# Attention scores as f32 products of four padded heads, and a generator built in four parts

## The chip, the cores and the metric

The kernel runs on one core of one Trainium2 chip. Its time is the device time of one execution in microseconds (us); the median of a few runs counts. The engines are TensorE (PE), VectorE (DVE), ScalarE (ACT) and GpSimd (POOL); SyncE (SP) issues most transfers. Each works through its own list in order, and semaphores tie the lists together.

## The reference

Two blocks follow each other on x of 16 sequences x 128 positions x 144 channels (C), with a condition vector of 144 for each sequence.

```python
# block 1: adaptive layer norm, attention with H = 16 heads of D = 9, MLP with FF = 576
ada = silu(c) @ W_ada + b_ada        # six vectors of 144 a sequence
h = layernorm(x) * (1 + scale_msa) + shift_msa
q, k, v = split(h @ W_qkv + b_qkv)
o = softmax(q * D**-0.5 @ k.T) @ v   # for each of the 16 heads
x = x + gate_msa * (o @ W_proj + b_proj)
h = layernorm(x) * (1 + scale_mlp) + shift_mlp
x = x + gate_mlp * (gelu(h @ W_fc1 + b_fc1) @ W_fc2 + b_fc2)
# block 2: rotation in the column space of P (144 x 64)
U, _ = qr(P)
A = skew(silu(cond) @ W.T + b)       # 64 x 64 from 2016 entries, for each sequence
z = x @ U
x = x + (z @ expm(A) - z) @ U.T
```

## The kernel before, in words

All weights and x stay in on-chip memory (SBUF). After a setup of about 33 us (loads, transposed W, the six vectors) one list of iterations b = -2 to 17 runs on every engine, each in four quarters q = 0 to 3. It is a software pipeline: iteration b transposes the input of sequence b + 2, makes q, k and v of b + 1 (`qkv`), the scores of b (`scores`), the exponentials and values of b - 1 (`scores_T`, `values`), and closes b - 2 (`sums`, `division`, `projection`, `gated`). Two other computations are threaded through the same iterations:

- **The QR of P**, as 64 steps of elimination on a matrix Z, four an iteration in 0 to 15. A step is a pair of products on TensorE that copy a row of Z to all partitions (`G_row` L1308, `B_row` L1313, with a selector that POOL makes), and nine small VectorE instructions (`eliminations`, L908 to L928), which use a root made by POOL. The next step's rows can only be made when Z is updated.
- **The matrix exponential of A**: entries (`windows` L1179, 252 tiny passes in iterations -1 and 0), `triangles`, `generator`, `scaled`, powers in iterations 2 to 4, halves in 5, odd part in 6, four squarings in 7 to 10 (`product`, L1171).

Scores: q and k are split into three bf16 parts and laid out in 64 columns a head (`qs`, `ks`), two heads a stack, transposed by TensorE (`stacks_T`, L1255) and copied by ScalarE (L622, L626). `scores` (L1263) forms four heads a quarter into one PSUM bank; VectorE takes their maximum (L984); the 16 maxima are again split in three and transposed (`NM`). `scores_T` forms the same scores transposed (L1273) and adds the negative maximum by a second product (L1274); ScalarE takes the exponential (L616). `values` (L1284) multiplies by v in 32-column groups. `sums` (L1292) adds the exponentials, VectorE takes 128 reciprocals (L944), `division` (L1300) spreads them, VectorE multiplies (L949), `projection` (L1318) ends it. Scores and transposed scores have a bank each (3 and 4).

```python
                for i in range(4):
                    dst = bank[4][:, 128 * i:128 * i + 128]
                    mm(dst, KT[parity][q // 2][:, q % 2, i, :], QT[parity][q // 2][:, i, :], start=True, stop=False)
                    ins = mm(dst, headsel[:, q % 2, 4 * (q // 2) + i, :], NMT[:, :], start=False, stop=True)
                ins.then_inc(s_ST, 1)
```

An f32 product appears as two TensorE instructions (passes) in the trace, a bf16 product or a transpose as one. After iteration 17 comes a last stage: M = expm(A) U^T, the MLP and the rotation.

## Time and profile before

| | us |
|---|---|
| median of 3 runs | 362.62 (361.86 to 363.21) |
| the profiled execution, its own time | 363.15 |
| its span, first to last instruction | 361.4 |
| TensorE busy | 318.2 (88%) |
| VectorE busy | 256.6 (71%) |
| ScalarE busy | 187.2 (52%) |
| POOL busy | 146.2 (40%) |
| mean granted TensorE clock | 0.948 of 2.4 GHz |

Busy time counts a matmul until its last result is in PSUM; matmuls overlap, so the distance between two starts tells what one costs in a stream, and the duration what a single reader waits for. What a stage costs is read by stretches of the span. The granted clock has two levels, 1.2 and 2.4 GHz, shown as 0.5 and 1.0 of full speed.

### The profile page before, as it was taken

The numbers are of one execution on the slowest core, as the hardware profiler recorded it, in microseconds if no ns is written. First come the engines' busy times: TensorE is split into PE (matmuls) and PEld (weight loads), VectorE is DVE, ScalarE is ACT, GpSimd is POOL, SyncE is SP. The second block draws the span as 40 slices with busy tenths as digits, with TensorE's granted clock in tenths as the row PEclk, the third lists the DMA queues.
The fourth block names the chain that finished last, engine by engine and source line by source line (L and its number), as shares of the span: only waits on it lengthen the run. The fifth ranks groups of instructions, "written<-read, shape, count | busy, mean of one in ns | idle before, by whom it ended". The sixth has DMA issues, their size and how long they took to land.

```text
span 361.4 us, 10608 instructions
## 1 busy us (share of the span) xinstructions
PE 318.2 (88%) x3935; PEld 245.4 (68%) x3935; DVE 256.6 (71%) x1063; ACT 187.2 (52%) x403; POOL 146.2 (40%) x421
## 2 busy tenths in 40 slices
PE   0598989889989899999999999999987957999995
PEld 0472668567877788787778777777776643467784
DVE  7381036688899989887786878988988576664243
ACT  1222464347766557567685676776762233623221
POOL 3512124235355454553543535545543508720000
PEclk9998765769999999999999999999999899999999
DMA  8817000000000000000000000000000000000013
GB/s 198 233 19 261 4 1 2 3 1 2 2 3 2 2 5 3 2 2 3 2 3 2 5 2 2 0 5 0 2 3 3 2 3 0 2 0 2 0 34 100
DMA packets 8765, 8.28 MB, mean 23 GB/s; under 512 B 1042, under 2 KB 8312, under 8 KB 8586
## 3 DMA queue, kind: packets, MB, share of 16 engines
q1 hardware_dynamic: 8006, 6.78, 6.5%
q10 hardware_dynamic: 708, 0.83, 0.8%
q8 instruction: 32, 0.52, 0.6%
q14 instruction: 19, 0.16, 0.2%
HBM read 6.40 MB, written 1.20 MB: 21 GB/s over the span
## 4 chain that ended last, share of the span: by engine, by line
PE 61%; DVE 18%; ACT 8%; issue 5%; POOL 4%; DMA 2%; ACTq 1%; DVEq 0%; POOLq 0%
PE bank L1255 5%; PE bank L1492 5%; PE bank L1284 4%; PE bank L1476 3%; PE bank L1318 3%; PE bank L1171 3%; PE bank L1273 3%; PE bank L1308 3%; PE bank L1300 3%; PE bank L1244 3%; PE bank L1245 2%; PE bank L1179 2%; PE bank L1274 2%; ACT KT L626 2%; PE bank L1263 2%
## 5 line engine op out<-in xcount | busy, mean ns | idle before, releaser
L440 POOL TENSOR_TENSOR root<-rec,mhalf 128x1 f32<-128x1 f32 x64 | 34.6, 540 | 107.5 <-DVE Z L922 107.5
L984 DVE TENSOR_REDUCE nmax<-bank 128x4 f32<-128x512 f32 x64 | 43.0, 672 | 34.5 <-PE bank L1263 34.2
L616 ACT ACTIVATE E<-bank 128x512 f32<-128x512 f32 x64 | 38.0, 594 | 40.6 <-PE bank L1274 40.2
L626 ACT ACTIVATE KT<-bank 64x512 bf16<-64x512 bf16 x64 | 37.5, 587 | 0.8
L1273 PE MATMUL bank<-QT,KT 128*128 128x128 bf16 x256 | 36.7, 224 | 0.0
L1274 PE MATMUL bank<-NMT,headsel 128*128 128x128 bf16 x256 | 36.3, 222 | 0.0
L1308 PE MATMUL bank<-Z,sel 128*128 128x128 f32 x128 | 29.5, 314 | 6.9 <-DVE Z L928 6.8
L1284 PE MATMUL bank<-E,V 128*32 128x128 f32 x512 | 27.9, 291 | 5.4 <-ACT E L616 5.4
L622 ACT ACTIVATE QT<-bank 128x512 bf16<-128x512 bf16 x32 | 19.0, 595 | 26.1 <-PE bank L1255 26.0
L1273 PEld LDWEIGHTS bank<-QT,KT 128*128 128x128 bf16 x256 | 24.3, 99 | 10.0 <-issue 10.0
L1308 PEld LDWEIGHTS bank<-Z,sel 128*128 128x128 f32 x128 | 20.9, 200 | 14.7 <-issue 13.6
L1263 PE MATMUL bank<-KT,QT 128*128 128x128 bf16 x256 | 25.8, 225 | 0.3 <-DVE nmax L984 0.3
L1274 PEld LDWEIGHTS bank<-NMT,headsel 128*128 128x128 bf16 x256 | 25.4, 99 | 0.2
L1313 PE MATMUL bank<-Z,sel 128*128 128x64 f32 x128 | 22.3, 257 | 1.3 <-DVE Z L928 1.3
L922 DVE SCALAR_TENSOR_TENSOR Z<-bank,cG,Z 128x128 f32<-128x128 f32 x64 | 22.2, 346 | 0.0
L1313 PEld LDWEIGHTS bank<-Z,sel 128*128 128x128 f32 x128 | 20.4, 201 | 1.4 <-DVE Z L928 1.4
L1300 PE MATMUL bank<-rsum,sumrow 128*128 128x128 f32 x128 | 18.5, 288 | 1.5 <-DVE rsum L944 1.5
L928 DVE SCALAR_TENSOR_TENSOR Z<-bank,cB,Z 128x64 f32<-128x64 f32 x64 | 18.2, 284 | 2.3
L434 POOL COPY sel<-ident 128x128 f32<-128x128 f32 x64 | 19.4, 305 | 0.0
L1318 PE MATMUL bank<-wproj,ON 128*128 128x144 f32 x128 | 19.1, 293 | 0.0
L1300 PEld LDWEIGHTS bank<-rsum,sumrow 128*128 128x128 f32 x128 | 15.5, 191 | 4.7 <-issue 3.0
L1492 PE MATMUL bank<-wfc2a,gT 128*128 128x144 f32 x128 | 18.6, 288 | 0.0
(270 smaller groups left out, 827.5 us busy)
## 6 DMA issues: line engine op xcount, KB each, us to landing
gates<-gates_dram SPq DMA_DIRECT2D x1, 2304.0 KB, 8.4
x_all<-in_x_dram SPq DMA_DIRECT2D x4, 288.0 KB, 7.6
out_dram<-x_all SPq DMA_DIRECT2D x8, 144.0 KB, 2.0
wskew<-in_L_cond_W_dram SPq DMA_DIRECT2D x4, 283.5 KB
wada<-in_L_cond_W_ada_dram ACTq DMA_DIRECT2D x1, 432.0 KB
wfc1a<-in_L_cond_W_fc_dram SPq DMA_DIRECT2D x1, 288.0 KB
wfc2a<-in_L_cond_W_fc_dram SPq DMA_DIRECT2D x1, 288.0 KB
wproj<-in_L_cond_W_proj_dram SPq DMA_DIRECT2D x16, 5.1 KB
```

What stands on the lines that cost most here:

```text
L440: link(nc.gpsimd.tensor_tensor(root[:, at], rec[:, at], mhalf[:, 0:1], ALU.pow))
L616: nc.scalar.activation(E[:, q, :, :].rearrange("p i t -> p (i t)"), bank[4][:, :], ACT.Exp).then_inc(s_E, 1)
L626: nc.scalar.activation(KT[parity][n][own, p, :, :].rearrange("p g t -> p (g t)"), bank[2][own, 256:512].bitcast(BF16), ACT.Copy).then_inc( ...
L984: nc.vector.tensor_reduce(nmax[:, q % 2, 4 * (q // 2):4 * (q // 2) + 4], bank[3][:, :].rearrange("p (i m) -> p i m", i=4), AX.X, ALU.max, ...
L1263: ins = mm(bank[3][:, 128 * i:128 * i + 128], QT[parity][q // 2][:, i, :], KT[parity][q // 2][:, q % 2, i, :], start=True, stop=True)
L1273: mm(dst, KT[parity][q // 2][:, q % 2, i, :], QT[parity][q // 2][:, i, :], start=True, stop=False)
L1274: ins = mm(dst, headsel[:, q % 2, 4 * (q // 2) + i, :], NMT[:, :], start=False, stop=True)
L1284: ins = mm(bank[5][own, cols], V[parity][:, head(q, i), :], E[:, q, i, :], start=True, stop=True)
L1300: ins = mm(bank[6][:, 128 * q:128 * q + 128], sumrow[:, q, :], rsum[:, :], start=True, stop=True)
L1308: mm(bank[7][:, 0:2 * RD], sel[:, n, :], Z[:, 0:2 * RD], start=True, stop=True).then_inc(s_Grow, 1)
L1313: mm(bank[7][:, 2 * RD:3 * RD], sel[:, n, :], Z[:, 2 * RD:3 * RD], start=True, stop=True).then_inc(s_Brow, 1)
L1492: mm(dst, gT[Q % 2][:, k, cols], wfc2a[:, k, :], start=(k == 0), stop=False)
```

## The change

- q and k are no longer split. Each head gets 32 columns (`SL`) in f32, four heads a stack. Column D of a head's k is 1; column D of q takes the negative maximum, so one product gives score minus maximum. `keys_T`, `queries_T` and, once the maxima are there, `queries_again_T` transpose four stacks each in f32. `scores` and `scores_T` make eight heads at a time, each head a product of 32 rows in its own row group and its own bank out of 0 to 3; both use the same four banks. VectorE takes two maxima of 1024 elements, ScalarE two exponentials of 1024, an iteration.
- v gets a column of ones, so that `values` yields the sums too. `sums` and `division` go; the result is transposed back (`heads_back`), divided in 16 reciprocals and one product (`divided`), transposed (`normalized_T`) and projected with two products instead of four.
- The elimination starts in iteration -2: four steps in -2, -1 and in even iterations, three in odd ones, one B step left in 16 (`STEPS`). Its products read the identity matrix instead of selectors. They share bank 7 with `heads_back` and `projection`, which therefore wait for the last step (`row_bank`).
- The entries of A are formed in four parts in iterations 0 to 3 (`windows(n)`, `triangles(n)`), the generator in 4, its scaling in 5, `any_over` and the powers from 6, halves in 9, odd part in 10, squarings in 11 to 14. All of it uses banks 4 and 5, which are also those of the stacks, so TensorE waits in `bank5_read` and `bank4_read` until they are read.
- POOL's selectors, its subtractions and its spreading of v go; `column_cleared` comes. POOL's addition of sequence b - 3 and its statistics move to quarter 0 of iteration b. W_proj is loaded by 3 transfers instead of 17, and 8 small setup operations go.
- ScalarE's order in an iteration is now: `queries_again`, `modulated`, the copy of the values, `stacked` (q, k, v), the first exponential, `keys_copied`, `queries_copied`, the generator's copies, the copies of the transposed output, the second exponential.

VectorE's order is now: maximum 0, step 0, statistics (quarter 0); step 1, `divided`, powers' sums (1); maximum 1, step 2, `normalized`, the generator's work (2); step 3, `gated` (3).

```diff
-    SL = 64
-    NP6 = 6 * D
+    SL = 32
...
+        qstk = [sb(f"qstk{p}", [128, H, SL]) for p in range(2)]
+        kstk = sb("kstk", [128, H, SL])
+        QT, QM = sb("QT", [128, 4, 128]), sb("QM", [128, 4, 128])
+        KT = [sb(f"KT{p}", [128, 4, 128]) for p in range(3)]
+        V = [sb(f"V{p}", [128, H, VS]) for p in range(3)]
+        E = sb("E", [128, 2, 4, 2, 128])
...
+        STEPS = {}
+        for b in range(-2, B + 1):
+            for q in range(4):
+                if len(STEPS) <= RD and (b < 0 or q < 3 or b % 2 == 0):
+                    STEPS[b, q] = len(STEPS)
+        assert len(STEPS) == RD + 1
...
+        PARTS, POWER, HALVES, ODD, SQUARE = 4, 6, 9, 10, 11
...
+            def column_cleared(b):
+                pool.wait_ge(s_qmT, b + 1)
+                nc.gpsimd.memset(qstk[b % 2][:, :, D:D + 1], 0.0).then_inc(s_qz, 1)
             def added(b):
-                wait(pool, s_pr, b + 2, s_apart[0])
-                xb = x_all[:, bass.ds(b, 1), :].rearrange("p a c -> p (a c)")
-                nc.gpsimd.tensor_tensor(xb, xb, tmp[:, :], ALU.add).then_inc(s_x1, 1)
+                pool.wait_ge(s_pr, b + 1)
+                nc.gpsimd.tensor_tensor(x_all[:, b, :], x_all[:, b, :], tmp[:, :], ALU.add).then_inc(s_x1, 1)
...
+            def queries_again(b):
+                act.wait_ge(s_qmT, b + 1)
+                wait(act, s_ST, 2 * b)
+                nc.scalar.activation(QM[:, :, :].rearrange("p j t -> p (j t)"), bank[5], ACT.Copy).then_inc(s_QM, 1)
...
+            def exponentials(b, g):
+                act.wait_ge(s_ST, 2 * b + g + 1)
+                wait(act, s_pv, 2 * b - 1 + g)
+                nc.scalar.activation(E[:, g, :, :, :].rearrange("p r j t -> p r (j t)"), scored(g), ACT.Exp).then_inc(s_E, 1)
...
+            def triangles(n):
+                first, last = 16 * n, min(16 * n + 16, RD - 1)
+                dve.wait_ge(s_LP, n + 1)
+                TT(A0[:, :, first:last].rearrange("p c i -> p i c"),
+                   bank[5][:, 0:(last - first) * NC].rearrange("p (i c) -> p i c", c=NC),
+                   lower[:, first:last].rearrange("p (i a) -> p i a", a=1).to_broadcast([128, last - first, NC]),
...
+            def maximum(b, g):
+                dve.wait_ge(s_S, 2 * b + g + 1)
+                wait(dve, s_qmT, b - 1)
+                nc.vector.tensor_reduce(qstk[b % 2][:, 8 * g:8 * g + 8, D:D + 1].rearrange("p (j r) a -> p r (j a)", r=4),
+                                        scored(g).rearrange("p r (j m) -> p r j m", j=2),
+                                        AX.X, ALU.max, negate=True).then_inc(s_max, 1)
...
+            def windows(n):
+                first, last = 16 * n, min(16 * n + 16, RD - 1)
+                pe.wait_ge(s_v, 4)
+                pe.wait_ge(s_KT, n + 2)
...
+            def generator_stage(b):
+                if 0 <= b < PARTS:
+                    windows(b)
+                if b == PARTS:
+                    pe.wait_ge(s_L, PARTS)
+                    pe.wait_ge(s_KT, b + 2)
+                    matrices_T(A0, 5, s_LTp)
+                if b == PARTS + 1:
+                    norms(b)
+                if b == PARTS + 2:
+                    any_and_replicas(b)
+                if power(b):
+                    powers(b)
+                if b == HALVES:
+                    high_halves(b)
+                if b == ODD:
+                    odd_part(b)
+                if squaring(b):
+                    squared(b)
...
+            def bank5_read(b):
+                wait(pe, s_KT, min(b + 2, B))
+                if 0 <= b < PARTS:
+                    pe.wait_ge(s_L, b + 1)
+                if b == PARTS:
+                    pe.wait_ge(s_rsq, 1)
+                if b == PARTS + 1:
+                    pe.wait_ge(s_Bs, 1)
+                if power(b):
+                    pe.wait_ge(s_N, b - POWER + 1)
+                if b == HALVES:
+                    pe.wait_ge(s_ev, 6)
+                if b == ODD:
+                    pe.wait_ge(s_X, 1)
+                    pe.wait_ge(s_Y, 1)
+                if squaring(b):
+                    pe.wait_ge(s_X, b - SQUARE + 2)
...
+            def stack_T(dst, stack, done):
+                for j in range(4):
+                    ins = pe.transpose(dst[:, 128 * j:128 * j + 128], stack[:, 4 * j:4 * j + 4, :].rearrange("p h s -> p (h s)"),
+                                       ident[:, :])
+                ins.then_inc(done, 1)
+            def keys_T(b):
+                pe.wait_ge(s_stk, 2 * b + 2)
+                wait(pe, s_QM, b - 1)
+                if b == 0:
+                    pe.wait_ge(s_v, 3)
+                stack_T(bank[5], kstk, s_kT)
+            def queries_T(b):
+                pe.wait_ge(s_stk, 2 * b + 2)
+                pe.wait_ge(s_V, b + 1)
+                wait(pe, s_qz, b - 1)
+                stack_T(bank[4], qstk[b % 2], s_qT)
+            def queries_again_T(b):
+                pe.wait_ge(s_max, 2 * b + 2)
+                stack_T(bank[5], qstk[b % 2], s_qmT)
...
+            def scores(b, g):
+                pe.wait_ge(s_QT, b + 1)
+                pe.wait_ge(s_KT, b + 1)
+                wait(pe, s_max, 2 * b + g)
+                wait(pe, s_E, 2 * b - 2 + g)
+                if b == 0:
+                    pe.wait_ge(s_v, 4)
+                for j in range(2):
+                    for r in range(4):
+                        rows = slice(32 * r, 32 * r + 32)
+                        ins = mm(bank[r][:, 128 * j:128 * j + 128], QT[rows, 2 * g + j, :], KT[b % 3][rows, 2 * g + j, :],
+                                 start=True, stop=True)
                 ins.then_inc(s_S, 1)
...
+            def scores_T(b, g):
+                pe.wait_ge(s_QM, b + 1)
+                pe.wait_ge(s_max, min(2 * b + 3 + g, 2 * B))
+                wait(pe, s_E, 2 * b + g)
+                for j in range(2):
+                    for r in range(4):
+                        rows = slice(32 * r, 32 * r + 32)
+                        ins = mm(bank[r][:, 128 * j:128 * j + 128], KT[b % 3][rows, 2 * g + j, :], QM[rows, 2 * g + j, :],
+                                 start=True, stop=True)
                 ins.then_inc(s_ST, 1)
...
+            def row_bank(k, b):
+                wait(pe, s_Gstep, min(k, RD))
                 wait(pe, s_Bstep, k - 1)
-                mm(bank[7][:, 0:2 * RD], sel[:, n, :], Z[:, 0:2 * RD], start=True, stop=True).then_inc(s_Grow, 1)
-            def B_row(k, n):
-                wait(pe, s_Bstep, k)
-                mm(bank[7][:, 2 * RD:3 * RD], sel[:, n, :], Z[:, 2 * RD:3 * RD], start=True, stop=True).then_inc(s_Brow, 1)
+            def heads_back(b):
+                pe.wait_ge(s_O, b + 1)
+                wait(pe, s_pr, b)
+                for n in range(2):
+                    cols = slice(128 * n, 128 * n + 128)
+                    ins = pe.transpose(bank[7][:, 256 + 128 * n:384 + 128 * n], Osb[:, cols], ident[:, :])
+                ins.then_inc(s_Ot, 1)
+            def normalized_T(b):
+                pe.wait_ge(s_on, b + 1)
+                pe.transpose(bank[5][:, 0:128], ON[:, 0:C1], ident[:, :])
+                pe.transpose(bank[5][0:C2, 128:256], ON[:, C1:C], ident[:, :]).then_inc(s_OnT, 1)
             def projection(b):
-                pe.wait_ge(s_on, b + 1)
-                for q in range(4):
-                    ins = mm(bank[6][:, 0:C], ON[:, q, :], wproj[:, q, :], start=(q == 0), stop=(q == 3))
-                ins.then_inc(s_proj, 1)
+                pe.wait_ge(s_oT, 2 * b + 2)
+                mm(bank[7][:, 256:256 + C], oT1[:, :], wproj1[:, :], start=True, stop=False)
+                mm(bank[7][:, 256:256 + C], oT2[:, :], wproj2[:, :], start=False, stop=True).then_inc(s_proj, 1)
...
+            def step(b, q, before=None):
+                k = STEPS.get((b, q))
+                if k is not None or before:
+                    last = k if k is not None else max([n for at, n in STEPS.items() if at < (b, q)]) + 1
+                    row_bank(last, b)
+                if before:
+                    before(b - 2)
+                if k is None:
+                    return
+                if k < RD:
+                    mm(bank[7][:, 0:2 * RD], ident[:, k:k + 1].to_broadcast([128, 128]), Z[:, 0:2 * RD],
+                       start=True, stop=True).then_inc(s_Grow, 1)
+                if k > 0:
+                    mm(bank[7][:, 2 * RD:3 * RD], ident[:, k - 1:k].to_broadcast([128, 128]), Z[:, 2 * RD:3 * RD],
+                       start=True, stop=True).then_inc(s_Brow, 1)
...
+            def attention(b):
+                if scoring(b):
+                    scores(b, 0)
+                if b >= 3:
+                    pe.wait_ge(s_pr, b - 2)
+                step(b, 0)
+                if closing(b):
+                    values(b - 2, 1)
+                if b == B + 1:
+                    transposed_again(0)
+                if prepares(b):
+                    qkv(b + 1)
+                if b == -1:
+                    generator_entries(3, 4)
+                if weighing(b):
+                    scores_T(b - 1, 0)
+                step(b, 1, heads_back if closing(b) else None)
+                if b == B + 1:
+                    transposed_again(1)
+                if prepares(b):
+                    keys_T(b + 1)
+                    queries_T(b + 1)
+                if b == B:
+                    U_parts(b, 0)
+                if scoring(b):
+                    scores(b, 1)
+                if weighing(b):
+                    values(b - 1, 0)
+                generator_stage(b)
+                if b == B:
+                    U_parts(b, 1)
+                if closing(b):
+                    pe.wait_ge(s_on, b - 1)
+                step(b, 2)
+                if closing(b):
+                    bank5_read(b)
+                    normalized_T(b - 2)
+                if b == B + 1:
+                    more_squarings()
+                    transposed_again(2)
+                if weighing(b):
+                    scores_T(b - 1, 1)
+                step(b, 3, projection if closing(b) else None)
+                if b == B + 1:
+                    transposed_again(3)
+                if scoring(b):
+                    if closing(b):
+                        pe.wait_ge(s_oT, 2 * b - 2)
+                    else:
+                        bank5_read(b)
+                    queries_again_T(b)
+                if normalizing(b):
+                    if b > -2:
+                        bank4_read(b)
+                    inputs_T(b + 2)
```

## Rows read from the trace of the kernel before

**Rows 1.** The page: busy time of TensorE; its granted clock in 40 slices

```profile
PE 318.2 (88%) x3935; PEld 245.4 (68%) x3935; DVE 256.6 (71%) x1063; ACT 187.2 (52%) x403; POOL 146.2 (40%) x421
...
PEclk9998765769999999999999999999999899999999
```

**Rows 2.** Stretches: start:end, us; busy us (instructions) of each engine; granted clock, DMA

```profile
47.10:63.30 16.20, 15.41 (x180) 12.66 (x178) 9.19 (x40) 8.40 (x18) 6.35 (x21) 0.61 0.01 2
63.30:82.80 19.50, 16.45 (x152) 12.01 (x151) 14.95 (x64) 7.65 (x18) 6.36 (x18) 0.71 0.01 2
...
95.90:110.70 14.80, 13.34 (x202) 10.87 (x200) 14.41 (x56) 9.80 (x22) 7.78 (x22) 1.00 0.01 3
...
154.20:214.10 59.90, 56.97 (x928) 47.47 (x925) 45.84 (x196) 41.62 (x93) 27.45 (x88) 1.00 0.01 2
214.10:265.80 51.70, 48.56 (x670) 39.46 (x667) 45.41 (x196) 36.70 (x83) 27.36 (x88) 1.00 0.01 2
265.80:299.00 33.20, 24.33 (x325) 19.18 (x326) 25.32 (x111) 10.88 (x21) 11.32 (x30) 0.95 0.01 2
```

**Rows 3.** The page's groups: line, operation, shapes, count; busy us, mean ns; idle before

```profile
L984 DVE TENSOR_REDUCE nmax<-bank 128x4 f32<-128x512 f32 x64 | 43.0, 672 | 34.5 <-PE bank L1263 34.2
L616 ACT ACTIVATE E<-bank 128x512 f32<-128x512 f32 x64 | 38.0, 594 | 40.6 <-PE bank L1274 40.2
...
L1318 PE MATMUL bank<-wproj,ON 128*128 128x144 f32 x128 | 19.1, 293 | 0.0
```

**Rows 4.** Timeline of TensorE in iteration 12: start us, us, operation, count

```profile
227.08 0.96 PE L1244 MATMUL bank<-wqkv,hT 128*128 128x432 f32 x2
...
228.60 0.45 PE L1308 MATMUL bank<-Z,sel 128*128 128x128 f32 x2
...
229.15 0.43 PE L1284 MATMUL bank<-E,V 128*32 128x128 f32 x8
229.39 1.06 PE L1292 MATMUL bank<-E,sumsel 128*32 128x128 f32 x32
230.38 0.23 PE L1273 MATMUL bank<-QT,KT 128*128 128x128 bf16 x1
...
230.84 0.39 PE L1263 MATMUL bank<-KT,QT 128*128 128x128 bf16 x4
231.06 0.44 PE L1308 MATMUL bank<-Z,sel 128*128 128x128 f32 x2
```

**Rows 5.** Timeline of TensorE in the last stage

```profile
306.40 1.02 PE L1476 MATMUL bank<-hT1q,wfc1a 128*128 128x512 f32 x2
...
307.57 1.14 PE L1482 MATMUL bank<-hT2q,wfc1r 17*128 17x512 f32 x8
...
350.60 0.66 PE L1504 MATMUL bank<-ident,x_all 128*128 128x128 f32 x4
351.09 0.27 PE L1505 MATMUL bank<-ident,x2r 128*128 128x128 f32 x1
```

**Rows 6.** Timeline of VectorE: an elimination's first instruction and what follows the elimination

```profile
229.26 0.17 DVE L908 RECIPROCAL rec<-bank 128x1 f32<-128x1 f32 x1
...
230.79 0.95 DVE L944 RECIPROCAL rsum<-bank 128x128 f32<-128x128 f32 x1
```

**Rows 7.** Timeline of TensorE in iterations -1 and 0

```profile
34.63 0.99 PE L1244 MATMUL bank<-wqkv,hT 128*128 128x432 f32 x2 [0.98 <-ACT hT L547]
...
46.80 0.63 PE L1263 MATMUL bank<-KT,QT 128*128 128x128 bf16 x4
47.22 1.75 PE L1244 MATMUL bank<-wqkv,hT 128*128 128x432 f32 x2
...
50.21 0.61 PE L1308 MATMUL bank<-Z,sel 128*128 128x128 f32 x2
50.74 1.10 PE L1179 MATMUL bank<-ident,v 16*64 16x8 f32 x32
```

**Rows 8.** VectorE's instructions grouped by line

```profile
L934 DVE TENSOR_TENSOR tmp<-bank,gates 128x144 f32<-128x144 f32 x16 | 4.8, 298 | 1.8 <-PE bank L1318 1.8
```

683 lines of the change are left out of this document (240 added, 443 removed).

## The prediction

> **What bounds the kernel now.** I read the page's busy times first: TensorE 318.2 us of 361.4, and its clock row, which shows where the granted clock was low [rows 1]. Then the busy times in stretches cut at the iterations [rows 2]. Iterations 0 to 14 take 218.7 us (47.1 to 265.8), iterations 15 to 17 take 33.2 us, the last stage 62.4 us, which the change leaves alone. In iterations 11 to 14 one takes 51.7 / 4 = 12.9 us, TensorE 94% busy, VectorE 88%; with squarings (7 to 10) 59.9 / 4 = 15.0 us. So TensorE sets the pace there and VectorE is close behind. Iterations 0 and 1 are dearer, 16.2 and 19.5 us: waits behind the generator, at a mean granted clock of 0.61 and 0.71.
>
> The timeline gives the price of each kind of product by starts, not by durations, which overlap [rows 4]: qkv 1.52 us; G and B rows 0.55 with the change of array shape behind them; four values products 0.24; 16 sums products 0.99, of which 0.85 is streaming and 0.14 the change back to full shape; eight bf16 products of scores_T 0.46; four of scores 0.22.
>
> **TensorE, per iteration.** *Removed:* sums, 0.99; division, four f32 products of 128 columns at 0.21 (below) and a change of shape, 1.0; half of the projection, 19.1 / 16 = 1.19 for eight passes [rows 3], so 0.5 saved; 32 bf16 products of scores_T (4 x 0.46 = 1.84), 16 of scores (0.88), 17 bf16 transposes at 0.055 (0.94). *Added:* 12 f32 transposes of stacks, four of heads and outputs. Four f32 transposes take 0.49 by starts, 0.66 with a tail of 0.17 [rows 5], so 0.12 each: 16 cost 1.8. The scores are now 16 f32 products with 32 rows, and scores_T 16 more. No such row exists, and two bounds stand around it. Bound above: each f32 product of 128 columns costs what one of full shape costs; a 512-column one takes 1.02 for its two passes, 0.85 without the tail [rows 5], so 128 columns 0.21, and 32 cost 6.8 us. Bound below: four in different row groups run at once. The nearest row speaks for that: L1482 does four products of 17 rows by 128, 512 columns, each into its own bank, in 1.14 us where one alone takes 1.02 [rows 5]. That is the new pattern itself, with other columns. I take 0.43 for eight, 1.7 for all 32. Values stay at 0.85. Changes of array shape go from 8 to about 11, at 0.1 to 0.14 each: +0.4. Sum: 12.1 busy before (94% of 12.9), less 6.2 removed, plus 1.8 + 1.7 + 0.4: **9.9 us**.
>
> The Trainium skill (TensorE: Matmul & The Clock Gate, "Measured speedup vs the span model") gives 3.07x, not 4x, for four row tiles. By that the 32 products would cost 2.2 us instead of 1.7, an estimate that would add under 0.5 us per iteration if all of it lay on the path. The trace agrees that there is an overhead, but shows 12% (1.14 against 1.02).
>
> **VectorE becomes the pace.** One elimination takes 1.53 us from its first instruction to the next work (229.26 to 230.79) [rows 6], and needs rows that TensorE makes only when the one before has finished. A maximum over 512 elements takes 0.67 [rows 3]; one over 1024 is bounded by 0.67 and 1.34; I take 1.15. The maxima's three-way split (four small operations) and the 128-wide reciprocal (0.95 [rows 6]) go; a reciprocal of 16 and a product of 144 remain, 0.55 together. The chain of an iteration with four steps: maximum 1.15, elimination 1.53, wait until TensorE has passed values, qkv, scores_T and heads_back and made the next rows 1.25, elimination 1.53, division 0.55, maximum 1.15, elimination 1.53, xn 0.3, wait for projection and rows 0.85, elimination 1.53, gated 0.3 (298 ns [rows 8]), less overlaps: **11.6**. With three steps it ends over TensorE: projection 0.5, queries_again_T 0.45, inputs_T 0.2, scores 0.45 and changes of shape behind the third elimination: **10.9**. Mean 11.25 against 12.9. ScalarE loses the copies of the bf16 split and keeps three stack copies of 512 columns out of six; its exponentials are two of 1024 elements, about 1.05 each (594 ns for 512 [rows 3]). That fits the gaps. POOL loses selectors and subtractions; VectorE's work hid them, so they give nothing. New waits: `statistics` now waits for POOL's addition, queued there behind a root and a masked column; that ends inside the 1.25 us in which VectorE waits for rows anyway, and would cost 0.3 outside it. `wait(s_pr)` ahead of step 0 holds values and qkv behind it, but gated ends before the maximum that covers it. SP's queue is shorter by 14 small weight loads, so the gates behind them land sooner; nothing on the path waits for them.
>
> **The generator's work now meets closed waits.** `bank5_read` stands ahead of `normalized_T`, so TensorE waits at once for what VectorE does at the end of quarter 2, and scores_T, projection and the fourth step are queued behind it. On top of 11.6 / 10.9: windows of 64 passes cost 2.1 (32 passes 1.1 [rows 7]) and triangles 0.3, before the third elimination: iterations 2 and 3 come to 14.6 and 13.7; 0 and 1, which close nothing, to 12.3 each. The generator's three operations (about 2 us) wait in full: 15.3 in iteration 4; scaling, 13.9 in 5. Powers add 1 us of TensorE, and first and second power 3 us of VectorE (14.41 busy in 95.9 to 110.7 against 45.41 / 4 = 11.35 [rows 2]): 12.7, 13.7, 14.8 in 6 to 8. Halves and odd part, 14.7 and 14.5. Squaring, 2 us of TensorE, delays the third elimination by 1.5: 12.6 mean in 11 to 14. Sum 24.6 + 28.3 + 29.2 + 41.2 + 29.2 + 50.4 = **202.9 against 218.7: -15.8**.
>
> **Start.** Eight eliminations move ahead of iteration 0, none of them covered. Each costs 1.53 plus 0.6 for its rows: four delay xn and the first hT, so qkv(0) comes at about 41.6, not 34.6 [rows 7]. The other four overlap qkv and the last entries. With four steps of 2.1 to 2.2 us, qkv and the last entries at the lower clock (3.0 and 3.4), and transposes, I get the first scores at 54, not 46.8: **+7**; with overlap of the entries at best +3. ScalarE's and POOL's setup (the headsel copy, KT memsets) was off this path.
>
> **End.** Iteration 15 has three steps and no preparation: 10.5. In 16 one B step is left; behind it U's parts and the 14-wide root as now; 17 is shorter by the 128-wide reciprocal and division. About 26.5 for all three against 33.2 [rows 2]: **-6.7**.
>
> Sum: 361.4 - 15.8 + 7 - 6.7 = 345.9. TensorE now has gaps of 2 to 4 us in iterations 2 to 10. The trace shows what the lower clock does: iterations 0 and 1, where TensorE waits or issues the tiny window products, have a granted clock of 0.61 and 0.71 of 2.4 GHz, and qkv takes 2.99 us (47.22 to 50.21) instead of 1.52 [rows 2, 4, 7]. At 1.2 GHz the pieces on the path (projection, queries, scores, rows) cost up to 2.2 more per iteration. I allow two or three such iterations beyond those of now, +5: span 350.9. The profiled run lies 1.75 above its span, the median 0.5 below that run: **352**.
>
> **Rivals.**
> *The clock* (ends slower). TensorE stays at 1.2 GHz through most of iterations -2 to 10. For: its idle share rises from 6% to 15 to 20%, and iterations 0 and 1 had 0.61 and 0.71. Against: iteration 3's stretch has 10% idle and 1.00. At 2.2 us each it decides from seven iterations on (347.1 + 7 x 2.2 = 362.5); twelve give 373. The Trainium skill (TensorE: Matmul & The Clock Gate, Part 1) says that idleness lets the clock fall to 1.2 GHz. Chance 0.17.
> *No overlap of row groups.* 6.8 instead of 1.7 us, 16 times 5.1 = 82, perhaps 15 hidden in gaps: 415. Against it stands L1482. 0.06.
> *The four shared banks.* Scores and scores_T use the same four banks four times an iteration, each after a maximum or an exponential; where these don't fit the gaps another 1 us per iteration is lost: 362 to 368. Before, scores and scores_T had a bank each. 0.10, half of it within 0.5%.
> *More.* The waits between eliminations overlap better and the clock holds: 1 us less per iteration, 330 to 340. 0.12.
> *Forecast:* 0.55, its own range 341 to 361.
>
> A difference under 0.5% (1.8 us) can't be told from none. Faster: 0.53 + 0.12 + 0.01; same: 0.08; slower: 0.26. The range leaves out the no-overlap case and half of the clock's: 338 to 370.
>
> **What would show it.** Right: eight scores products in about 0.6 us with their tail; TensorE busy under 90% in 11 to 14, with iterations of 12.6 us and its waits on VectorE; first scores near 54; waits of TensorE for VectorE ahead of projection and normalized_T. Wrong: scores passes that start 0.1 us apart; a clock under 0.85 over the span; iterations 0 and 1 over 14 us.

## The result and the profile after

379.25 us, median of 4 runs (378.27 to 379.55), against 362.38 of the kernel before beside it: ratio 1.046, 95% interval 1.043 to 1.049. 352 was forecast, within 338 to 370. The profiled execution took 379.3 us, span 377.5. In all ratios below, executions over 1.5% above a kernel's fastest are left out as slow: three of e3's four and two of e12's seven.

The page of the changed kernel: busy time of the engines and the granted clock in 40 slices.

```profile
PE 304.5 (81%) x3471; PEld 221.1 (59%) x3471; DVE 227.7 (60%) x966; ACT 130.4 (35%) x274; POOL 92.6 (25%) x279
...
PEclk9978587887696988899999696999999986999999
```

Every engine is busy for less time than before [rows 1] and the kernel takes longer. The clock row says where to look: dips up to slice 25 and at 33 and 34, where before they ended with slice 9 but for one. The mean granted clock is 0.890, before 0.948; as the engine has two levels (1.2 and 2.4 GHz), that is 2 x 0.110 x 377.5 = 83 us at the lower one against 2 x 0.052 x 361.4 = 38.

The same execution cut at the first scores of iterations 0, 2, 6, 9, 11 and 15 and at the first product of the last stage: start:end, us; busy us (instructions) of each engine; granted clock, DMA.

```profile
56.70:84.80 28.10, 23.66 (x305) 18.35 (x304) 18.97 (x86) 8.16 (x18) 7.19 (x25) 0.80 0.01 2
84.80:153.80 69.00, 55.67 (x703) 42.67 (x702) 39.72 (x164) 23.96 (x53) 14.05 (x49) 0.80 0.01 2
153.80:195.50 41.70, 35.05 (x511) 26.57 (x510) 31.47 (x127) 19.59 (x43) 10.45 (x36) 0.99 0.01 2
195.50:231.60 36.10, 28.77 (x373) 22.12 (x372) 21.39 (x87) 12.23 (x27) 7.41 (x26) 0.83 0.01 1
231.60:285.70 54.10, 49.54 (x799) 38.35 (x798) 34.76 (x149) 27.97 (x60) 14.33 (x50) 0.99 0.01 2
285.70:314.20 28.50, 17.35 (x233) 12.33 (x232) 20.34 (x96) 9.55 (x19) 10.23 (x25) 0.89 0.01 1
314.20:377.50 63.30, 58.63 (x412) 39.95 (x412) 31.55 (x100) 20.25 (x41) 16.78 (x33) 0.96 0.07 20
```

Against the terms of the prediction (its sum 345.9, before the 5 us allowed for the clock):

| stretch | forecast | measured | off |
|---|---|---|---|
| to the first scores | 54 | 56.7 | +2.7 |
| iterations 0, 1 | 24.6 | 28.1 | +3.5 |
| 2 to 5 | 57.5 | 69.0 | +11.5 |
| 6 to 8 | 41.2 | 41.7 | +0.5 |
| 9, 10 | 29.2 | 36.1 | +6.9 |
| 11 to 14 | 50.4 | 54.1 | +3.7 |
| 15 to 17 | 26.5 | 28.5 | +2.0 |
| last stage | 62.4 | 63.3 | +0.9 |

These differences add up to 31.7 us, and 18.4 of them are in the six iterations 2 to 5, 9 and 10: 105.1 us against 86.7. They are those in which `bank5_read`, ahead of `normalized_T` (L1310), waits for VectorE. Timeline of TensorE in iteration 9, at the start of the second half of its work: start us, us, operation, count, idle time before.

```profile
205.56 0.49 PE L1329 MATMUL banks<-Z,ident 128*128 128x128 f32 x2
205.88 0.33 PE L1332 MATMUL banks<-Z,ident 128*128 128x64 f32 x2
209.43 0.45 PE L1310 MATMUL banks<-ident,ON 128*128 128x128 f32 x1 [3.22 <-issue]
...
210.02 1.24 PE L1275 MATMUL banks<-QM,KT 32*128 32x128 f32 x16
211.19 0.85 PE L1315 MATMUL banks<-wproj,oT 128*128 128x144 f32 x2
...
212.31 1.06 PE L1231 MATMUL banks<-ident,qstk 128*128 128x128 f32 x4
...
213.73 1.24 PE L1263 MATMUL banks<-KT,QT 32*128 32x128 f32 x16
```

The wait shows as a gap of 3.22 us ("issue": the profile names no releaser). Behind it everything runs at half speed: sixteen passes of scores_T take 1.24 us where they take 0.73 in iteration 13, and from `normalized_T` to the next scores are 4.30 us. The gaps ahead of L1310 are 2.3, 2.3, 4.1, 4.1, 3.2 and 3.2 us in the six iterations, 19.2 in all, and at most 0.3 in the others.

The start of a single profile is to be read with care: the first scores come at 56.7 us here, but between 53.9 and 56.7 in the six profiled kernels that share this start (this one, e1, e2, e6, e8, e9).

### The profile page after: what moved, and what is told of

It is laid out like the page before. It is cut to its first block, busy times and chain, and to the rows that moved or that the text cites. A ratio compares the mean times of both kernels' runs of the same rounds, so it can differ in the third digit from the quotient of the medians.

```text
span 377.5 us, 9229 instructions
## 1 busy us (share of the span) xinstructions
PE 304.5 (81%) x3471; PEld 221.1 (59%) x3471; DVE 227.7 (60%) x966; ACT 130.4 (35%) x274; POOL 92.6 (25%) x279
## 4 chain that ended last, share of the span: by engine, by line
PE 67%; DVE 18%; issue 9%; POOL 2%; DMA 2%; ACT 1%; ACTq 1%; DVEq 0%
PE banks L1329 6%; PE banks L1231 5%; PE banks L1481 4%; PE banks L1275 4%; PE banks L1226 4%; PE banks L1263 4%; PE banks L1465 3%; PE banks L1088 3%; PE banks L1227 3%; PE banks L1289 3%; PE banks L1332 3%; PE banks L1315 2%; DVE Z L840 2%; PE banks L1099 2%; DMA p<-in_L_cond_P_dram 2%
## 5 line engine op out<-in xcount | busy, mean ns | idle before, releaser
L900 DVE TENSOR_REDUCE qstk<-banks 128x8 f32<-128x1024 f32 x32 | 39.0, 1220 | 12.7 <-PE banks L1263 9.7
L1329 PE MATMUL banks<-Z,ident 128*128 128x128 f32 x128 | 31.9, 335 | 15.3 <-DVE Z L846 9.9
L517 ACT ACTIVATE E<-banks 128x1024 f32<-128x1024 f32 x32 | 32.8, 1025 | 14.2 <-PE banks L1275 14.0
L1329 PEld LDWEIGHTS banks<-Z,ident 128*128 128x128 f32 x128 | 21.8, 212 | 23.2 <-DVE Z L840 11.8
L1275 PE MATMUL banks<-QM,KT 32*128 32x128 f32 x512 | 26.0, 322 | 3.5 <-issue 3.5
L1263 PE MATMUL banks<-KT,QT 32*128 32x128 f32 x512 | 26.0, 322 | 0.0
L1231 PE MATMUL banks<-ident,qstk 128*128 128x128 f32 x128 | 22.7, 308 | 1.6 <-issue 1.6
L1332 PE MATMUL banks<-Z,ident 128*128 128x64 f32 x128 | 23.7, 272 | 0.0
L1310 PE MATMUL banks<-ident,ON 128*128 128x128 f32 x16 | 5.7, 354 | 20.6 <-issue 16.5
L1332 PEld LDWEIGHTS banks<-Z,ident 128*128 128x128 f32 x128 | 22.1, 216 | 0.2 <-DVE tmp L853 0.2
L840 DVE SCALAR_TENSOR_TENSOR Z<-banks,cG,Z 128x128 f32<-128x128 f32 x64 | 22.2, 347 | 0.0
L1289 PE MATMUL banks<-E,V 128*32 128x128 f32 x512 | 21.1, 283 | 0.6 <-ACT E L517 0.6
L547 ACT ACTIVATE oT<-banks 128x128 f32<-128x128 f32 x16 | 4.4, 278 | 42.3 <-PE banks L1311 42.0
```

Source lines behind the costliest of these rows:

```text
L517: nc.scalar.activation(E[:, g, :, :, :].rearrange("p r j t -> p r (j t)"), scored(g), ACT.Exp).then_inc(s_E, 1)
L840: STT(Z[:, 0:2 * RD], bank[7][:, 0:2 * RD], cG[:, kk], Z[:, 0:2 * RD], ALU.mult, ALU.add).then_inc(s_Gstep, 1)
L900: nc.vector.tensor_reduce(qstk[b % 2][:, 8 * g:8 * g + 8, D:D + 1].rearrange("p (j r) a -> p r (j a)", r=4), scored(g).rearrange("p r (j m ...
L1231: ins = pe.transpose(dst[:, 128 * j:128 * j + 128], stack[:, 4 * j:4 * j + 4, :].rearrange("p h s -> p (h s)"), ident[:, :])
L1263: ins = mm(bank[r][:, 128 * j:128 * j + 128], QT[rows, 2 * g + j, :], KT[b % 3][rows, 2 * g + j, :], start=True, stop=True)
L1275: ins = mm(bank[r][:, 128 * j:128 * j + 128], KT[b % 3][rows, 2 * g + j, :], QM[rows, 2 * g + j, :], start=True, stop=True)
```

## The experiments

Beside each is the kernel before on the same chip; ratios are to it.

**e1: the wait moved behind the work that doesn't need it.**

```diff
 def normalized_T(b):
-    pe.transpose(bank[5][:, 0:128], ON[:, 0:C1], ident[:, :])
-    pe.transpose(bank[5][0:C2, 128:256], ON[:, C1:C], ident[:, :]).then_inc(s_OnT, 1)
+    pe.transpose(bank[6][:, 256:384], ON[:, 0:C1], ident[:, :])
+    pe.transpose(bank[6][0:C2, 384:512], ON[:, C1:C], ident[:, :]).then_inc(s_OnT, 1)
...
 if closing(b):
-    bank5_read(b)
     normalized_T(b - 2)
...
 if scoring(b):
-    if closing(b):
-        pe.wait_ge(s_oT, 2 * b - 2)
-    else:
-        bank5_read(b)
+    bank5_read(b)
     queries_again_T(b)
```

ScalarE's copies (L547, L548) read bank 6 accordingly, and `queries_again_T` no longer waits for them (`s_oT`); in the timeline above it follows the projection without a gap, so that wait cost nothing that shows.

> Changed kernel, with the output of normalized_T in bank 6 (columns 256 to 511) and not in bank 5, and bank5_read moved from ahead of normalized_T to ahead of queries_again_T in every iteration. Theory A (the waits in bank5_read idle TensorE 2.3 to 4.1 us in iterations 2 to 5, 9 and 10, 19.0 us in all, and its granted clock falls behind them): the wait comes later and shorter, TensorE has normalized_T, scores_T, projection and the B row before it, iterations 2 to 5, 9 and 10 fall from 105.1 us to some 85 to 90, the time to 360 to 365. Theory B (the row-tiled products or the windows themselves are what costs): 375 to 379, since neither is touched. If only the clock were cured and not the direct wait, or the reverse: 368 to 372.

Measured: 363.91 us (10 runs, 361.61 to 364.99), ratio 1.001 (0.998 to 1.004), 15 us less than the changed kernel. Its stretches of iterations 2 to 5, 6 to 8, and 9 and 10:

```profile
82.46:140.58 58.12, 52.35 (x703) 40.11 (x702) 39.58 (x164) 23.74 (x53) 14.03 (x49) 0.87 0.01 2
140.58:186.36 45.78, 38.67 (x511) 28.81 (x511) 31.48 (x127) 19.76 (x43) 10.42 (x36) 0.89 0.01 2
186.36:213.78 27.42, 23.68 (x369) 18.03 (x368) 21.03 (x86) 11.97 (x27) 7.24 (x25) 1.00 0.01 2
```

The six iterations take 85.5 us, just under the forecast's 86.7, not 105.1. Theory A holds. But 6 to 8, which the edit doesn't touch, take 45.8 us where they took 41.7: their clock is now 0.89 and was 0.99. The lower clock didn't go everywhere: where it left some iterations, it came up in others. The edit shortens the waits and lifts the clock at once, so e1 alone can't say which of the two gave the gain.

**e2: the waits kept, but filled.** Idle matmuls keep TensorE at work in the gaps and shorten nothing. They multiply the identity matrix by 256 columns of a weight and write what nobody reads.

```diff
 if closing(b):
+    for _ in range({2: 5, 3: 5, 4: 9, 5: 9, 9: 7, 10: 7}.get(b, 0)):
+        mm(bank[6][:, 256:512], ident[:, :], wqkv1[:, 0:256], start=True, stop=True)
     bank5_read(b)
     normalized_T(b - 2)
```

> Changed kernel with idle matmuls (ident by 256 columns of wqkv1, into bank 6 columns that nobody reads) put ahead of the bank5_read wait: 5 in iterations 2 and 3, 9 in 4 and 5, 7 in 9 and 10, sized by the gaps of 2.3, 4.1 and 3.2 us at 0.43 us each. No wait is made shorter. Theory A1 (half of the loss is the clock that falls after the gap): granted clock stays at 2.4 GHz from the gap to the maximum, 2.5 to 3 us saved in each of six iterations, 362 to 368. Theory A2 (the loss is the direct wait, the clock little): 377 to 382. Theory B: 377 to 382 too.

Measured: 375.44 us, ratio 1.032 (1.027 to 1.037): 3.8 us gained. The same place in iteration 9, and then the stretches of iterations 2 and 3, 4 and 5, 6 to 8, and 9 and 10:

```profile
205.80 3.24 PE L1403 MATMUL banks<-wqkv,ident 128*128 128x256 f32 x14
209.19 0.30 PE L1310 MATMUL banks<-ident,ON 128*128 128x128 f32 x1
...
209.53 0.73 PE L1275 MATMUL banks<-QM,KT 32*128 32x128 f32 x16
210.20 0.50 PE L1315 MATMUL banks<-wproj,oT 128*128 128x144 f32 x2
...
211.53 0.73 PE L1263 MATMUL banks<-KT,QT 32*128 32x128 f32 x16
```

```profile
84.58:118.89 34.31, 33.70 (x417) 26.30 (x416) 18.16 (x78) 11.77 (x27) 6.78 (x24) 0.83 0.01 2
118.89:149.47 30.58, 29.64 (x343) 22.89 (x343) 21.49 (x86) 11.98 (x27) 7.24 (x25) 1.00 0.01 2
...
149.47:195.25 45.78, 39.20 (x511) 29.05 (x510) 31.48 (x127) 19.75 (x43) 10.42 (x36) 0.89 0.01 2
195.25:226.21 30.96, 29.77 (x397) 23.12 (x396) 20.81 (x84) 11.98 (x27) 7.24 (x25) 1.00 0.01 2
```

`normalized_T` begins as late as before, yet is 2.34 us ahead of the next scores, not 4.30. In 4, 5, 9 and 10 the clock is at its upper level throughout, and they take 61.5 us, 3.1 over the forecast's 58.4; so full waits at full clock had been sized nearly right. The six iterations give back 9.2 us, less than the 15 or more that A1 expected, since in 2 and 3 the clock is still low (0.83). Iterations 6 to 8 take 4.1 us of it away again.

Three kernels now separate the two parts in iterations 4, 5, 9 and 10: 69.7 us in the changed kernel, 61.5 with the waits filled, and 54.4 with them moved (e1: 27.4 for 9 and 10 above, and for 4 and 5 the row that follows). So in these four the clock behind the waits costs 8.2 us, and the waits themselves 7.2.

```profile
113.65:140.58 26.93, 22.20 (x307) 16.61 (x306) 21.34 (x86) 11.77 (x27) 7.25 (x25) 0.99 0.01 2
```

Iterations 2 and 3 are another matter. In the changed kernel's iteration 2, the time up to the fall of the clock and the time at the lower level; the last work before the wait; then e2's clock in the same place:

```profile
92.60:96.20 3.60, 3.60 (x101) 3.24 (x100) 2.41 (x7) 0.88 (x2) 0.87 (x3) 1.00 0.02 5
96.20:103.00 6.80, 4.50 (x32) 3.69 (x32) 2.30 (x14) 1.45 (x3) 0.94 (x3) 0.50 0.00 0
...
93.85 2.03 PE L1099 MATMUL banks<-ident,v 16*64 16x8 f32 x64
...
98.92 0.44 PE L1310 MATMUL banks<-ident,ON 128*128 128x128 f32 x1 [2.30 <-issue]
```

```profile
95.90:99.30 3.40, 3.40 (x12) 2.77 (x11) 2.10 (x11) 0.00 (x0) 0.94 (x3) 0.50 0.00 0
99.30:103.00 3.70, 3.70 (x47) 3.01 (x48) 0.89 (x6) 1.90 (x4) 0.00 (x0) 1.00 0.00 0
```

TensorE is busy without a gap until 96.6 us, yet the clock falls at 96.2, before the wait begins. With the wait filled it falls in the same place and rises again some 3.5 us sooner. So this wait can lengthen the lower clock, but it doesn't bring it down. Just before the fall stand the 64 tiny passes of `windows` (L1099). They are a rival as a cause that no run took alone, and they can't be enough by themselves: in e11 below the same passes of iterations 2 and 3 pass without a fall.

**e3 and e4: the eliminations back from iterations -2 and -1**, in the changed kernel and in e1's.

```diff
-for b in range(-2, B + 1):
+for b in range(0, B + 1):
     for q in range(4):
-        if len(STEPS) <= RD and (b < 0 or q < 3 or b % 2 == 0):
+        if len(STEPS) <= RD:
             STEPS[b, q] = len(STEPS)
```

> Changed kernel with the eliminations back to four in each iteration from iteration 0 on (none in -2 and -1). The prediction priced the move ahead at +7 us before the first scores and a gain of 1.5 us in each odd iteration; measured +9.9 before the first scores. If the eliminations ahead are uncovered: first scores at 47 to 49, odd iterations longer by up to 1.5 us each where VectorE sets the pace (8 of them), so 371 to 379. If VectorE is not what sets the pace (TensorE at half clock does): first scores 47 to 49 and the iterations as they are, 368 to 371.

> Both edits (normalized_T in bank 6 with the wait later; eliminations four an iteration from 0 on). With the waits gone VectorE should set the pace, so the fourth elimination of odd iterations should cost its 1.5 us: the sum of both gains less some 5 us, 352 to 360. If the two are independent 350 or less; if the loss has another cause than both, over 370.

Measured: e3 376.54 us (370.28 to 377.33, four runs too scattered for a ratio); e4 354.53 us, ratio 0.972 (0.967 to 0.978), so 9.4 below e1 and within its expectation. The profile of e3 is that of its 377.33 us. TensorE ahead of the first scores, first in the changed kernel, then in e3:

```profile
38.96 0.76 PE L1329 MATMUL banks<-Z,ident 128*128 128x128 f32 x2 [2.07 <-DVE Z L846]
...
41.85 0.77 PE L1329 MATMUL banks<-Z,ident 128*128 128x128 f32 x2 [1.80 <-DVE Z L846]
...
44.74 0.76 PE L1329 MATMUL banks<-Z,ident 128*128 128x128 f32 x2 [1.38 <-DVE Z L846]
...
45.62 1.75 PE L1226 MATMUL banks<-wqkv,hT 128*128 128x432 f32 x2
...
56.74 1.24 PE L1263 MATMUL banks<-KT,QT 32*128 32x128 f32 x16
```

```profile
35.50 0.99 PE L1226 MATMUL banks<-wqkv,hT 128*128 128x432 f32 x2 [0.99 <-ACT hT L475]
...
42.24 0.73 PE L1263 MATMUL banks<-KT,QT 32*128 32x128 f32 x16
```

The move ahead costs 56.7 - 42.2 = 14.5 us in these two profiles, and 13.8 as the mean of all six with the eliminations ahead (55.7) against the six with none (41.8; e3, e4, e5, e10, e11, e12). That is twice the 7 forecast, and e3's own expectation (first scores at 47 to 49) missed it too. In the rows, eliminations are 2.9 us apart where 2.1 to 2.2 had been taken. That the start lost only 9.9 is because the changed kernel without the move would begin its scores 4.6 us before the old one. What the move gives back lies behind: from iteration 0 to 14 are 235.4 us in e3 and 229.0 in the changed kernel, 217.4 in e4 and 213.3 in e1; from there to the end 97.8 against 91.8, and 96.8 against 92.9. So the move costs 13.8 and returns 8.0 with e1's shorter waits. In the changed kernel the two profiles give 14.5 and 12.4, but the return is in doubt: e3's fastest run, 370.28 us at a clock of 0.897 and not 0.868, is 9.0 below the changed kernel, which would leave a return of some 5.5 if it started like the profiled one. So e3 doesn't tell its two expectations apart.

**e7: four eliminations ahead instead of none or eight.** `range(-1, B + 1)`, four in each iteration but three in 2, 6, 10 and 14, on e1.

> The kernel of e1 (normalized_T in bank 6) with the eliminations from iteration -1 on: four there, four in the others but three in iterations 2, 6, 10 and 14. Moving all eight to iteration 0 and on took 13.8 us from the time before the first scores and gave 4.1 and 3.9 us back behind it. If the four of iteration -1 lie beside the wait for inputs and for the copies there: first scores near 41 to 44 and two to four us less behind them, 350 to 354. If each elimination ahead is on the path with 1.5 us or more: first scores 47 to 48, 356 to 360.

Measured: 355.34 us, ratio 0.980 (0.977 to 0.984): between its two expectations, and no gain on e4 (354.53, and 354.41 when timed again below). The four lie beside waits, as the first expectation had it (first scores at 42.9), but gain little behind: 217.0 us in iterations 0 to 14 (217.4 in e4) and 94.0 from there to the end (96.8).

**e6: the order of the row groups**, in scores and, with the same edit, scores_T of the changed kernel.

```diff
-for j in range(2):
-    for r in range(4):
-        rows = slice(32 * r, 32 * r + 32)
+for r in range(4):
+    rows = slice(32 * r, 32 * r + 32)
+    for j in range(2):
```

> Changed kernel with the eight products of scores and scores_T ordered by row group (both products of one group of 32 partitions behind each other) and not round robin over the four groups. Theory that products of different row groups overlap and those of one don't: 16 passes take longer than the 0.73 us measured, near twice, and four calls an iteration in 16 iterations cost some 0.5 us each where TensorE is on the path, 20 us or more, 395 to 415. If the order doesn't matter: 379. If the order now is the dear one: below 375.

Measured: 378.41 us, ratio 1.046 (1.042 to 1.050). One call, in this kernel and in the changed one:

```profile
262.49 0.75 PE L1263 MATMUL banks<-KT,QT 32*128 32x128 f32 x16
```

```profile
265.13 0.73 PE L1263 MATMUL banks<-KT,QT 32*128 32x128 f32 x16
```

The order doesn't matter. In both traces the first four passes have started within 0.04 us (265.13 to 265.16 here) and the next follow 0.2 us after the first: the four row groups run beside each other in either order. What a call would take without that overlap no run shows.

**e8 and e9: what sets the pace in iterations 11 to 14.** e8 adds two idle matmuls (0.86 us) ahead of the squares in each; e9 forms two of the sixteen squares of each product and leaves the rest of the squaring out.

```diff
 # e8
+for _ in range(2 if 11 <= b <= 14 else 0):
+    mm(bank[6][:, 256:512], ident[:, :], wqkv1[:, 0:256], start=True, stop=True)
 generator_stage(b)
 # e9, with product(bk, lhs, rhs, n=NC) over c in range(n)
-product(5, Ym, Xm)
-product(4, Xm, Ym).then_inc(s_Xp, 1)
+product(5, Ym, Xm, 1)
+product(4, Xm, Ym, 1).then_inc(s_Xp, 1)
```

> Changed kernel with two idle matmuls (0.43 us each, 0.86 us) ahead of the squares in iterations 11 to 14, where no wait in bank5_read is for VectorE and the clock is 2.4 GHz. The prediction had VectorE set the pace there (12.6 us an iteration; 13.5 measured). If TensorE's own work is the path there: each of the four grows by 0.8 to 0.9 us, 3.3 to 3.6 us in all, 382.5 to 383. If VectorE sets the pace: no change, 379 to 380.

> Changed kernel with two of the sixteen squares of each of the two products in iterations 11 to 14 (8 passes where 64 stood, some 1.8 us less TensorE work an iteration); the rest of the squaring is left out, the copies and waits stay. It asks what the attention itself now takes in an iteration without generator work, to stand beside 12.9 us in the kernel before. If TensorE sets the pace (0.7 us came from 0.86 us of idle products): some 1.4 us less, 12.1 us an iteration, 373 to 374 in all. If VectorE's chain as the prediction had it (11.6 and 10.9 us in turn) is then the pace: 11.3 us, 370 to 371. If the attention itself has gained nothing by the change: 12.9 us or more, 376.5 to 379.

Measured: 384.13 us (383.33 to 384.99), above both expectations, and 374.05 us (371.46 to 376.05), beside the first. Iterations 11 to 14 of e8, then of e9:

```profile
230.85:287.81 56.96, 53.58 (x816) 40.98 (x815) 34.83 (x150) 27.98 (x60) 14.31 (x50) 0.99 0.01 2
```

```profile
231.08:278.70 47.62, 43.05 (x575) 31.85 (x574) 34.83 (x150) 27.97 (x60) 14.30 (x50) 0.99 0.01 2
```

The squares of iteration 13, with the wait ahead of them, and the rows of the third elimination behind them, in the changed kernel:

```profile
266.72 1.15 PE L1088 MATMUL banks<-Xm,Ym 64*64 64x64 f32 x32 [0.29 <-ACT QT L493]
...
268.73 0.49 PE L1329 MATMUL banks<-Z,ident 128*128 128x128 f32 x2
```

From 266.72 to the rows at 268.73 are 2.01 us; in e9's iteration 11 it is 0.38 (238.93 to 239.31). So e9 takes 2.01 - 0.38 = 1.63 us out ahead of each third elimination's rows, 6.5 in all, and the four iterations are 6.5 shorter. e8 puts 0.86 in, of which some 0.16 fill the wait for ScalarE, and each is 0.7 longer, 2.8 in all. So what TensorE does ahead of these rows counts in full. The rest of e8's extra 4.9 us lies behind: from iteration 15 to the end are 95.0 us at a clock of 0.85, against 91.8 at 0.94, with the same work. With an eighth of the squares an iteration takes 47.62 / 4 = 11.9 us; before, without squares, 12.9 [rows 2]. The attention itself gained 1.0 us an iteration, not the 1.65 of the forecast.

**e5, e10, e11, e12: the tail.** In e4 the clock is at its lower level for most of iterations 15 to 17. e5 fills the waits there.

```diff
+def idle(b, n):
+    for _ in range(n if b >= B - 1 else 0):
+        mm(bank[5][:, 0:256], ident[:, :], wqkv1[:, 0:256], start=True, stop=True)
...
+if b <= B:
+    idle(b, 2)
 step(b, 1, heads_back if closing(b) else None)
```

The same stands ahead of steps 2 and 3; in iteration 17 two ahead of transposed_again(1), three ahead of more_squarings and three behind transposed_again(3).

> The kernel of e4 (normalized_T in bank 6, four eliminations an iteration from 0 on) with idle matmuls (0.43 us each, into bank 5, read by nobody) in the waits of iterations 15 to 17: two at each of seven places, three at two more. In e4 the granted clock is at 1.2 GHz from 268.3 to 295.6 us, and from the first scores of iteration 15 to the end are 96.8 us against 91.8 in the changed kernel. If the clock there is what the gaps of 0.8 to 1.6 us make of it: the stretch falls back to 90 to 92 us, the time to 347 to 351. If it is not the gaps: no gain, or 1 to 3 us longer by the idle matmuls that don't fit their gaps, 354 to 358.

Measured: 350.75 us, ratio 0.967 (0.962 to 0.972). e4 and e5 were then timed again on one chip:

> The kernel of e4 once more, beside that of e5 on one chip, since the two were timed in different sessions (354.5 and 350.8) and their runs overlap (351.6 to 356.6 against 349.4 to 353.9). If the idle matmuls of the tail gain: this one 353 to 356, at least 2 us above the other. If the difference was one of sessions: the two within 1 us.

> The kernel of e5 once more, beside that of e4. If the idle matmuls gain by the clock in iterations 15 to 17: 349 to 352. If not: within 1 us of the other.

Measured: 354.41 us for e4's kernel, ratio 0.980 (0.975 to 0.985), and for e5's 351.6 (median of the five counted), ratio 0.970 (0.967 to 0.973). Up to the first scores of iteration 15 the two profiled executions agree in every iteration (213.4 us each); then, in e11 and in e12:

```profile
255.65:293.20 37.55, 27.82 (x277) 19.41 (x277) 23.71 (x111) 9.53 (x19) 14.86 (x35) 0.64 0.01 2
255.65:352.40 96.75, 82.50 (x648) 56.60 (x647) 53.22 (x205) 29.69 (x60) 27.76 (x60) 0.85 0.04 13
```

```profile
253.38:290.90 37.52, 30.36 (x325) 21.66 (x325) 26.31 (x119) 11.75 (x23) 16.77 (x38) 1.00 0.01 2
253.38:346.70 93.32, 82.36 (x688) 57.76 (x687) 53.38 (x205) 29.80 (x60) 27.86 (x60) 0.99 0.05 14
```

The fill lifts the clock from 0.64 to 1.00 and saves 3.4 us from there to the end, under the 5 to 7 expected; the medians are 2.8 apart. This is the fastest version: about 3% faster than the kernel before.

**e10: a gap at the start filled as well.** It adds to e5 four idle matmuls ahead of the fourth elimination's rows in iteration 0, where e5 waits 1.8 us.

> The kernel of e5 with four more idle matmuls ahead of the fourth elimination's rows in iteration 0, where TensorE waited 1.8 us (50.1 to 51.9) and the clock then was at 1.2 GHz from 51.2 to 58.1 us. If the gap is what the clock falls behind: iteration 0 and 1 together 1 to 3 us shorter than 26.3, time 348 to 350. If the fall there comes from the stretch's small products and not from the gap: 350 to 352.

Measured: 354.68 us, ratio 0.977 (0.971 to 0.982). Iterations 0 and 1 came to 25.2 us at clock 0.95 instead of 26.3 at 0.80, but iterations 2 to 5 then ran at 0.84 and not 0.96 and took 60.4 instead of 56.0. The kernel is slower than e5, outside both expectations. Whether the filling did that is open: e4 has the same 0.84 in iterations 2 to 5 with nothing filled anywhere, as the next rows show.

**The price of the clock.** The cleanest is from one kernel seen twice. Iterations 2 to 5 of e4 and of e11, whose kernel is the same:

```profile
66.28:126.66 60.38, 54.99 (x711) 42.53 (x710) 42.72 (x184) 24.02 (x53) 16.22 (x56) 0.84 0.01 2
```

```profile
68.50:124.46 55.96, 48.63 (x711) 37.41 (x710) 42.52 (x184) 23.95 (x53) 16.13 (x56) 0.96 0.01 2
```

Their iterations 2 and 3 alone, in e4 and in e11:

```profile
66.28:98.01 31.73, 30.68 (x401) 24.24 (x400) 19.50 (x87) 12.01 (x27) 7.68 (x28) 0.77 0.01 2
```

```profile
68.50:96.48 27.98, 25.60 (x401) 20.17 (x401) 18.82 (x84) 11.77 (x27) 7.52 (x27) 0.95 0.01 2
```

The lower level held for 2 x 0.16 x 60.38 = 19.3 us in one and 2 x 0.04 x 55.96 = 4.5 in the other, and 14.8 us more of it cost 4.4: 0.3 us each. The Trainium skill (TensorE: Matmul & The Clock Gate, "HAM oscillation — how this bites in real kernels") reckons half of the throttled time as lost. Here it is 0.3 in this stretch, 8.2 of some 22 us, 0.37, in the four iterations of e2, and 3.4 of some 27 us, 0.13, in the tail. That TensorE is only part of the path would explain prices under a half; no run shows it by itself.

## Why the prediction was wrong

**The step that failed** is the last of the sum, the clock: "I allow two or three such iterations beyond those of now, +5". The mechanism was named, as the first rival, and its price of 2.2 us an iteration was fair: e2 gives back 2.0 in each of 4, 5, 9 and 10. Its extent was taken too small. The closed waits of `bank5_read` were added to the path as waits, but the half speed of what is queued behind them was not, and the clock was at its lower level behind all six. Over the whole span the lower level held 45 us longer than before (83 against 38). At the prices found, 0.13 to 0.37 us each, that is 6 to 17 us, an estimate, where 5 was allowed.

How far this is shown: of the 18.4 us by which the six iterations exceed their term, filling the gaps gives 9.2 back (e2), though the kernel as a whole gained only 3.8, as iterations 6 to 8 ran at a lower clock instead. Of the other 9.1, 3.1 are the waits themselves in 4, 5, 9 and 10, and 6.0 are in 2 and 3, where the clock is still low. At most some 3.7 of these 6.0 can be put down to the clock by analogy: e4 and e11 differ by that much in iterations 2 and 3 (31.7 and 28.0 us) at 0.77 and 0.95. The rest is open. The terms themselves are not clean either: by the prices named, 2.1 and 0.3 on top of 11.6 and 10.9, iterations 2 and 3 come to 14.0 and 13.3 us, not to 14.6 and 13.7, and the miss there would be 1.0 us larger.

**The start** was the right idea at half its size: +7 forecast for the eliminations ahead, 14 measured. The first `qkv` comes at 45.6 us in the changed kernel and at 35.5 in e3, 10.1 us for what had been put at 7 (41.6 against 34.6): the rows shown are 2.9 us apart instead of 2.2, at the lower clock. From there to the first scores the changed kernel takes another 4.4 us more (11.1 against 6.7), where the forecast had nothing. Against it goes an earlier start that the forecast had put at nothing: without the move the changed kernel would begin its scores 4.6 us before the old one (42.2 against 46.8). The setup that went had been called "off this path"; which part of it gives the 4.6 no run shows. So the net +9.9 for +7 comes from two errors that partly cancel, which is luck.

**"VectorE becomes the pace"** was wrong. The chain of work that ended last runs, from 258.4 to 272.5 us, on VectorE for some 3 of 14 us: the last elimination of iteration 12 with `gated`, and the third of iteration 13. The other eliminations and both maxima are off it. TensorE was busy 49.54 of 54.10 us in 11 to 14, 92%, where under 90% had been forecast, and an iteration took 13.5 us for 12.6: 3.7 us in all. The sum for TensorE had one term too small. It took 0.43 us by starts for eight of the new products, and the trace has 0.65 (below), which is 0.9 us more in an iteration with 32 of them. That it is these 0.9 that the four iterations are over is argued from the size, not tested. The maximum of 1024 elements (1.15 taken) and the exponential (1.05) measured:

```profile
L900 DVE TENSOR_REDUCE qstk<-banks 128x8 f32<-128x1024 f32 x32 | 39.0, 1220 | 12.7 <-PE banks L1263 9.7
...
L517 ACT ACTIVATE E<-banks 128x1024 f32<-128x1024 f32 x32 | 32.8, 1025 | 14.2 <-PE banks L1275 14.0
```

**Right:** that row-tiled products overlap. A call of eight takes 0.65 to the next start and 0.73 with its tail, against 0.43 and 0.6 forecast, where eight at the full-shape price of 0.21 would be 1.7, and the passes of the four row groups start together (e6). TensorE's busy time fell from 318.2 to 304.5 us in spite of the lower clock. Iterations 6 to 8 (+0.5) and the last stage stood, and the end came within 2 us (28.5 for 26.5). Of the rivals, no overlap is excluded; the four shared banks can be no more than a part of the 0.65 us that an iteration without most squares is over its forecast (11.9 for 11.25), and no run took them apart from the dearer products. The rival of the clock had it low through most of iterations -2 to 10; from the first scores to iteration 10 it was low for 30% of the time (mean 0.85).

Of the signs, first scores near 54 (53.9 to 56.7) and the idle ahead of `normalized_T` were seen; TensorE under 90% and 12.6 us in 11 to 14 were not. Of the signs of being wrong, iteration 0 over 14 us (14.5) was seen, iteration 1 was not (13.6). The clock under 0.85 was not (0.89): as a mean over the whole span, that bound was too low to warn.

What stays open is what brings the clock down. In iterations 4, 5, 9 and 10 it fell during or just behind a wait of 3.2 to 4.1 us and stayed up when the wait was filled. In 2 and 3 it fell before the wait began. In the tail of e4 and e11 it fell behind gaps of 0.8 to 1.1 us. Iterations 6 to 8 had 0.99 in one kernel and 0.89 in another with the same work.

## What to carry to other kernels

Price a new wait of the busiest engine twice: the wait, and the half speed of what is queued behind it. In the four iterations where both could be measured, the wait cost 7.2 us and the half speed 8.2. Before accepting such a wait, ask which instructions behind it don't need it: moving one wait behind four operations, at the cost of 256 columns of another bank, was worth 15 us of 379, of both kinds together. Work pulled ahead of a pipeline's start is on the path with its full round trip there, at the clock of the start. It has to earn that back later; here eight eliminations cost 14 us and, once the waits were shorter, earned 8.

## What the runs showed of the hardware

Idle matmuls in waits gained time twice (3.8 us in e2; 3.4 us in the tail of e12 against e11), though they shorten no wait; in a third place (e10) nothing was gained. In iterations 15 to 17 of e11 the clock fell behind gaps of 0.8 to 1.1 us, with TensorE busy 6.41 of the 10.25 us before, and it stayed low for 27.3 us with gaps of 0.5 to 1.6 us; with most of these gaps filled it was 1.00 throughout. In iteration 2 of the changed kernel it fell while TensorE was busy without a gap. The same kernel ran one stretch at 0.84 and at 0.96 in two executions, 4.4 us apart, which is more than many edits are worth: compare stretches only beside their clock. Eight f32 products of 32 rows by 128 columns take 0.65 to 0.68 us by starts, whether products of different row groups or of the same one stand next to each other in the program.
